# Slot-to-token combine weights made among the small experts and stored, instead of in the combine's turns

## What is computed

```python
logits = einsum('bmd,npd->bmnp', x, phi_n)              # token m, slot n*16+p
D = softmax(logits, axis=1)                             # over the tokens: what a slot reads
C = softmax(logits.reshape(b, m, n * p), axis=-1)       # over the slots: what a token reads back
Xs = einsum('bmd,bmnp->bnpd', x, D)
hdn = layernorm(Xs) @ w1 + b1; hdn = gelu(hdn); Ys = hdn @ w2 + b2
Y = einsum('bsd,bms->bmd', Ys, C); h = h + Y
```

## Time and profile before

| | us |
|---|---|
| median of 3 runs | 1556.29 |
| lowest, highest | 1554.89, 1559.04 |
| profiled execution, its own time | 1558.22 |
| span of that execution in the trace | 1556.5 |
| e0 with PE at work | about 400 to 928 |
| combine with PE at work | about 939 to 1391 |

### The profile page before, as it was taken

The page is one execution under the profiler, slowest core; times in us unless marked ns, Lnnn a source line. Parts: engine busy times, 40 slices in busy tenths (PEclk is TensorE's granted clock), DMA queues, the critical chain, the costliest instruction groups (busy, mean ns, idle before and its releaser), DMA issues. The chain is left out here.

```text
span 1556.5 us, 28510 instructions
## 1 busy us (share of the span) xinstructions
PE 1431.4 (92%) x8824; PEld 1269.1 (82%) x8824; DVE 978.6 (63%) x2877; ACT 891.0 (57%) x1833; POOL 270.8 (17%) x255
## 2 busy tenths in 40 slices
PE   3899999985899999999999986999999999957995
PEld 1577777774799999999999976999999999956985
DVE  6776666442777777777777744777776777632231
ACT  1377777774666666666666642655555555524551
POOL 5411100000111111111111101122121212120434
PEclk9999999998899999999999997889898989867998
DMA  7035655576466666666666654434333436105542
GB/s 198 25 123 146 146 135 135 140 172 149 136 200 186 193 189 196 187 190 197 189 189 190 199 155 148 129 108 126 114 125 99 121 116 190 31 11 148 134 91 20
DMA packets 202698, 220.87 MB, mean 142 GB/s; under 512 B 30065, under 2 KB 169528, under 8 KB 202606
## 3 DMA queue, kind: packets, MB, share of 16 engines
q1 hardware_dynamic: 170254, 179.96, 41.5%
q10 hardware_dynamic: 24672, 32.79, 6.2%
q0 software_dynamic: 7680, 6.95, 2.4%
HBM read 142.27 MB, written 79.90 MB: 143 GB/s over the span
## 5 line engine op out<-in xcount | busy, mean ns | idle before, releaser
L1062 PE MATMUL bank<-e_w,e_h_full 128*128 128x192 f32 x1920 | 324.5, 326 | 0.3
L1062 PEld LDWEIGHTS bank<-e_w,e_h_full 128*128 128x128 f32 x1920 | 310.6, 190 | 1.2 <-ACT e_h_full L1123 0.8
L1123 ACT ACTIVATE e_h_full<-bank,e_b 128x512 f32<-128x512 f32 x240 | 165.1, 689 | 196.7 <-PE bank L60 196.7
L1000 POOL TENSOR_TENSOR e_ln_rstd<-e_ln_var_eps,minus_half 128x4 f32<-128x4 f32 x64 | 64.8, 1013 | 524.2 <-DVE e_ln_var_eps L1173 524.2
L1180 DVE TENSOR_SCALAR e_rows<-e_slot_sums,e_ln_mean_var,e_ln_rstd 128x192 f32<-128x192 f32 x256 | 79.9, 376 | 76.2 <-POOL e_ln_rstd L1000 76.2
L1096 ACT ACTIVATE e_x_full<-bank,e_ln_shift,e_ln_gain 128x512 f32<-128x512 f32 x128 | 92.6, 773 | 53.3 <-PE bank L1035 48.5
L585 DVE TENSOR_REDUCE column_neg_max<-bank 128x4 f32<-128x512 f32 x64 | 44.3, 692 | 115.1 <-PE bank L60 103.7
L1351 POOL TENSOR_TENSOR ln_rstd<-ln_var_eps,minus_half 128x2 f32<-128x2 f32 (+1 forms) x35 | 51.8, 1481 | 345.5 <-DVE ln_var_eps L1652 345.5
L60 PE MATMUL bank<-e_x_hi,e_w1hi 128*128 128x512 f32 x240 | 105.4, 439 | 5.3 <-DVE e_w1lo L1159 3.5
L830 PE MATMUL bank<-x,dispatch_weights 128*128 128x193 f32 x512 | 97.0, 333 | 14.1 <-ACT slot_stage L690 13.5
L1412 PE MATMUL bank<-slot_out_and_one,combineT 128*128 128x193 f32 x512 | 94.5, 338 | 10.9 <-DMA slot_out_and_one<-slot_outputs 10.9
(11 more groups left out here) (214 smaller groups left out, 3071.5 us busy)
## 6 DMA issues: line engine op xcount, KB each, us to landing
slot_sums<-slot_stage SPq DMA_DIRECT2D x64, 386.0 KB
e_slot_sums<-slot_sums SPq DMA_DIRECT2D x64, 386.0 KB, 3.6
slot_outputs<-e_stage ACTq DMA_DIRECT2D x64, 384.0 KB, 3.4
slot_out_and_one<-slot_outputs SPq DMA_DIRECT2D x32, 768.0 KB
e_w<-in_w SPq DMA_DIRECT2D x64, 288.0 KB, 3.0
slot_logits<-kept_logits SPq DMA_DIRECT2D x64, 256.0 KB
slot_logits<-slot_logits SPq DMA_DIRECT2D x32, 512.0 KB, 3.4
e_w1raw<-in_w SPq DMA_DIRECT2D x80, 192.0 KB, 2.7
```

The source lines that it names most:

```text
L1000: pool.tensor_tensor(rs[u][:], ve[u][:], half[:], ALU.pow).then_inc(rstd_ready, 1)
L1062: last = pe.matmul(ybank(u)[:, j // 2, (j % 2) * D:(j % 2 + 1) * D], hf[:, k, js], w2s[u][:, k, :], start=k == 0, stop=k == MT - 1)
L1123: act.activation(hf[:, m, :], hbank(u, m), act_fn, bias=b1s[:, m, ds(n, 1)]).then_inc(acted, 1)
```

## The change

A new class `Weigher` makes the combine weights of batch i in round i of e0: SP loads logits and maxima one round ahead, DVE adds the negated maximum behind the outputs of the even expert, ACT takes the exponential at the end of its odd expert, and in the next round's even expert, behind `take_x`, ACT's queue stores the tile (512 KB) to a new tensor `T["cw"]`. All its tiles have one buffer. The combine loads the finished weights, into two buffers. The diff at its core:

```diff
+class Weigher:
+    def load(self, sp, b):
+        past(sp, self.less, b)
+        sp.dma_start(self.lg[:], self.T["lg"][ds(b, 1), :, :, :]...).then_inc(self.lg_in, 16)
+        sp.dma_start(self.nmb[:], self.T["nm_rows"][ds(b, 1), :]....partition_broadcast(P)).then_inc(self.lg_in, 16)
+
+    def less_max(self, dve, b):
+        dve.wait_ge(self.lg_in, 32 * b + 32)
+
+        past(dve, self.stored, 16 * b)
+        dve.tensor_tensor(self.cw[:], self.lg[:], self.nmb[:].unsqueeze(1).broadcast_to([P, NC, P]), ALU.add
+                          ).then_inc(self.less, 1)
+
+    def exp(self, act, b):
+        act.wait_ge(self.less, b + 1)
+        act.activation(self.cw[:], self.cw[:], ACT.Exp).then_inc(self.exped, 1)
+
+    def store(self, act, b):
+        act.wait_ge(self.exped, b + 1)
+        act.dma_start(self.T["cw"][ds(b, 1), :, :, :]..., self.cw[:]).then_inc(self.stored, 16)
...
 class CombineLoads:
     def sync(self, sp):
-        for u in range(3):
-            sp.wait_ge(self.T["kept_stored"][u], 16 * ((NG * NC + 2 - u) // 3))
-        sp.wait_ge(self.T["nm_stored"], 16 * NG)
+        sp.wait_ge(self.T["cw_stored"], 16 * 2)
         for b in range(2):
-            self.load_logits(sp, b)
+            self.load_weights(sp, b)
     def scalar(self, act):
         act.activation(self.Whi[:], self.Wraw[:], ACT.Copy).then_inc(self.W_hi_ready, 1)
-        act.wait_ge(self.C_ready, 1)
-        act.activation(self.cT[:], self.lg[0][:], ACT.Exp).then_inc(self.C_exp, 1)
     def vector(self, dve):
-        dve.wait_ge(self.lg_in[0], 32)
-        dve.tensor_tensor(self.lg[0][:], self.lg[0][:], ..., ALU.add).then_inc(self.C_ready, 1)
...
 expert_phase, SP:
+                    if weigh is not None and (not isinstance(i, int) or i + 1 < turns):
+                        weigh.load(sp, i + 1)
 expert_phase, ACT, at the end of each expert of a round:
+                        if weigh is not None and u == 1:
+                            weigh.exp(act, i)
+                        if weigh is not None and u == 0 and (not isinstance(i, int) or i > 0):
+                            weigh.store(act, i - 1)
 expert_phase, ACT, behind the last round:
                 send(n_exp - 1, 1)
+                if weigh is not None:
+                    weigh.store(act, turns - 1)
+                    act.wait_ge(weigh.stored, 16 * turns)
                 if then is not None:
                     then.scalar(act)
 expert_phase, DVE, behind the outputs:
+                        if weigh is not None and u == 0:
+                            weigh.less_max(dve, i)
...
 combine_phase:
-                def load_logits(b):
-                    past(sp, S["C_exp"], b - 1)
-                    early.load_logits(sp, b)
+                def load_weights(b):
+                    past(sp, S["Y_done"], b - 1)
+                    early.load_weights(sp, b)
-                        pe.wait_ge(S["C_exp"], y + 1)
+                        pe.wait_ge(cT_in[u], 16 * (y // 2 + 1))
-                    if n is not None:
-                        exp_combine(n)
-                    if n is not None:
-                        less_max(n)
```

More of the change, by code:

```diff
@@ L152, in tower_program @@
                 expert_phase(nc, T, "e0", small, T["ys"].rearrange("s b d -> (s b) d"), ins["b2_0"], ACT.Gelu, al,
-                             then=early)
+                             then=early, weigh=Weigher(Alloc(nc, c3), al, T))
                 tower_sems.free_sems()
@@ L210, in load_first_weights, with __init__, wait_logits @@
             self.load_w2(sp, u, u)
+class Weigher:
+    def __init__(self, sb_of, sem_of, T):
+        self.T = T
+        self.lg, self.nmb = sb_of.sb("weigh_logits", [P, NC, P]), sb_of.sb("weigh_neg_max_rows", [P, P])
+        self.cw = sb_of.sb("weigh_out", [P, NC, P])
+        self.lg_in, self.less, self.exped = sem_of.sem("weigh_logits_in"), sem_of.sem("weigh_less_max"), sem_of.sem("weigh_exp")
+        T["cw_stored"] = self.stored = sem_of.sem("weigh_stored")
+    def wait_logits(self, sp):
+        for u in range(3):
+            sp.wait_ge(self.T["kept_stored"][u], 16 * ((NG * NC + 2 - u) // 3))
+        sp.wait_ge(self.T["nm_stored"], 16 * NG)
+    def load(self, sp, b):
+        past(sp, self.less, b)
+        sp.dma_start(self.lg[:], self.T["lg"][ds(b, 1), :, :, :].rearrange("a p c t -> p (a c) t")).then_inc(self.lg_in, 16)
+        sp.dma_start(self.nmb[:], self.T["nm_rows"][ds(b, 1), :].rearrange("a t -> (a t)").partition_broadcast(P)
+                     ).then_inc(self.lg_in, 16)
+    def less_max(self, dve, b):
[8 more added lines that the diff above has]
+        act.wait_ge(self.exped, b + 1)
+        act.dma_start(self.T["cw"][ds(b, 1), :, :, :].rearrange("a p c t -> p (a c) t"), self.cw[:]).then_inc(self.stored, 16)
 class CombineLoads:
@@ L219, in __init__ @@
         self.T, self.ins = T, ins
-        self.lg = [sb(f"slot_logits{u}", [P, NC, P]) for u in range(2)]
-        self.nmb = [sb(f"token_neg_max_rows{u}", [P, P]) for u in range(2)]
+        self.cT = [sb(f"combineT{u}", [P, NC, P]) for u in range(2)]
         self.Wraw = sb("Wqkv", [P, 2, 3 * D])
@@ L225, in __init__, with load_weights @@
         self.rank, self.numbers = sb("rank", [P, NE1]), sb("token_numbers", [P, NB])
-        self.cT = sb("combineT", [P, NC, P])
         self.W_in, self.tables_in, self.router_in = sem("qkv_weights_in"), sem("attn1_tables_in"), sem("router_in")
-        self.lg_in = [sem(f"slot_logits_in{u}") for u in range(2)]
+        self.cT_in = [sem(f"combine_weights_in{u}") for u in range(2)]
         self.W_hi_ready, self.W_split = sem("W_hi_ready"), sem("W_split")
-        self.C_ready, self.C_exp = sem("C_ready"), sem("C_exp")
         self.Wp0, self.Wp1 = sb("Wproj0", [P, D]), sb("Wproj1", [DR + 1, D])
         self.rw0, self.rw1 = sb("router0", [P, NE1]), sb("router1", [P, NE1])
-    def load_logits(self, sp, b):
-        sp.dma_start(self.lg[b % 2][:], self.T["lg"][b]).then_inc(self.lg_in[b % 2], 16)
-        sp.dma_start(self.nmb[b % 2][:], self.T["nm_rows"][b, :].partition_broadcast(P)).then_inc(self.lg_in[b % 2], 16)
+    def load_weights(self, sp, b):
+        sp.dma_start(self.cT[b % 2][:], self.T["cw"][b]).then_inc(self.cT_in[b % 2], 16)
     def sync(self, sp):
@@ L869, in past, with expert_phase @@
             eng.wait_ge(sem, value)
-def expert_phase(nc, T, name, L, dst, b2, act_fn, sem_of, routed_to=None, then=None):
+def expert_phase(nc, T, name, L, dst, b2, act_fn, sem_of, routed_to=None, then=None, weigh=None):
     n_exp, hid, MT, src, ln = L.n_exp, L.hid, L.MT, L.src, L.ln
@@ L985, in _ @@
                 load_rows(3, 1)
+                if weigh is not None:
+                    weigh.wait_logits(sp)
+                    weigh.load(sp, 0)
                 each_pair(sp, turn)
@@ L1411, in turn @@
                         for c in range(NC):
-                            last = pe.matmul(bank[:, 0, 0:D + 1], cT[:, c, :], ysb[u][:, c, :],
+                            last = pe.matmul(bank[:, 0, 0:D + 1], cT[u][:, c, :], ysb[u][:, c, :],
                                              start=c == 0, stop=c == NC - 1)
@@ L1500, in _ @@
             def _(act):
-                def exp_combine(b):
-                    act.wait_ge(S["C_ready"], b + 1)
-                    past(act, S["Y_done"], b)
-                    act.activation(cT[:], lg[b % 2][:], ACT.Exp).then_inc(S["C_exp"], 1)
                 def turn(t, u, n, y, q, a, p, r, z, w):
@@ L1563, in _ @@
                 st = Steps(dve, steps)
-                def less_max(b):
-                    dve.wait_ge(lg_in[b % 2], 32 * (b // 2 + 1))
-                    dve.tensor_tensor(lg[b % 2][:], lg[b % 2][:], nmb[b % 2][:].unsqueeze(1)
-                                      .broadcast_to([P, NC, P]), ALU.add).then_inc(S["C_ready"], 1)
                 def choose(r):
```

14 lines of the change are left out of this document (7 added, 7 removed).

## The result

The changed kernel takes 1681.64 us (median of 4 runs, 1678.95 to 1684.8) against 1557.64 for the kernel before (4 runs): ratio 1.0799 [1.0772, 1.0826]. A second set of runs gave 1677.95 (6 runs) against 1564.66 (21 runs): 1.075 [1.071, 1.079]. The change makes the kernel slower by 7.5 to 8%. The forecast was 1663, with 1628 to 1710 as its range.

A forecast was written before the change was run, and what follows sets the result against it. PE was taken to bound both e0 and the combine. Terms 78 + 26 + 3 = 107 us on the profiled 1558.22 gave 1665, or 1663 us for a median lying 1.9 lower; range 1628 to 1710.

The forecast's parts named there:

- The chain over ACT: e0: two table loads and the exponential on ACT delay PE's third part 2.5 us in 31 rounds, 78 us.
- The clock: e0: half of PE's new waits pull its clock down, 1.7 us lost each; 26 us, bounds 0 and 53.
- The combine: Combine's turns: the removed addition and exponential both have cover, so nearly nothing is gained; 0 to -3 us, taken as 0.
- its own condition: Combine: the prediction calls itself wrong if the combine's length changes by more than 5 us.
- The bound: Combine: if all PE's idle time came back, the gain would be 389.00 - 385.56 = 3.4 us.
- The end of e0: End of e0: `Wqkv_hi` stands behind the last store's landing, moving the combine's first loads 2.4 to 4 us; 3 taken.
- The addition and the store: e0, DVE: addition covered by the longer round (5 us without it); store landing taken as 4.0 us, so 0.
- the first rival: e0: ACT's table loads delay PE, with the clock falling in some rounds; 1634 to 1690 us, chance 0.62.
- the second (the store): e0: the store's landing decides; at 5 us 31 more, 1694, at 5.5 us 1710; chance 0.18.
- the third (a switch that costs more than its load): e0, ACT: the engine must first run empty; at twice 1.28 us a switch, 213 more, 1769 us; chance 0.05.
- The fourth (loads that hide): e0: one of the two loads runs while ACT waits for PE; 1596 us, up to 1630; chance 0.10.
- The fifth: Faster: ACT's waiting swallows the added work, the combine loses the exponential ahead of `x4T_hi`, 34 less, 1525 us; chance 0.03.

The follow-up runs named there:

- the fill experiment: Changed kernel with 5 more 128x512 matmuls, results unused, on PE in its wait between second and third part of the even expert: 1648.56 us, e0 612.1.
- the second profile: The changed kernel as it is, profiled again in a second set of runs: median 1677.95 us, e0 657.3.
- the second tile: Changed kernel with a tile of its own for the differences, so DVE's addition no longer waits for the store: 1677.38 us, e0 657.1.
- the small exponential: Changed kernel with e0's exponential on 128 of the 1024 numbers of a partition, both table loads a round kept: 1603.02 us, e0 593.4.

## Why the forecast held, and where its sum was off

The step that decided, two table loads and the exponential between two experts with PE's third part behind them, is shown: the loads are at their place, the wait is there 31 times, without loads it all but goes (5.3 us in 16 waits), and it shrinks with a shorter exponential by what that saves. The terms, against the earlier trace rows and the table of stages:

- **The chain over ACT: 78 us forecast, 72 to 75 measured.** 75.4 by the fill experiment, 119.3 - 47.7 = 71.6 in the changed kernel. A round loses 2.3 to 2.4 us where 2.5 was said. The 0.1 us in it for a matmul behind a wait was read from rows without one; behind the waits it is about right (0.50 to 0.53 us against 0.40).
- **The clock: 26 forecast, 44 to 50 measured.** This is the term that was mis-sized. 97 us at the lower level are 48.7 lost, 1.0 of which was there before; 50 in the second profile; 43.9 by the fill. The price of a fall (1.7 us, from the earlier trace rows) was right, the count wasn't: "half of the waits" are nearly all. The row of 4.54 us at one end and the idle 1.17 us in a window of 4 at the other leave 2.2 us open. The runs fill it: in them the clock fell behind no wait of up to 1.6 us, and behind nearly every one of 2.0 us or more.
- **The combine: 0 forecast (0 to -3), -7.8 and -6.4 measured, 7 of it at equal clock.** This step failed, and its own condition (a change of more than 5 us) says so. "The addition runs while POOL takes its power, and DVE still waits behind it" was read as cover for every turn, but the earlier trace rows have that wait only 16 times. In the turns that place tokens DVE has no wait behind the addition, so all of it delays what follows, and those turns take 11.79 us with it and 11.25 without: 6.5 us in 13. (The exponential's cover held: the combine is 469.5 us without it.) The bound was wrong as well, since the earlier trace rows cover 389 of the stage's 468.6 us: in all of it PE is busy for 433.79 us, so idle for 34.8, and for 431.37 of 460.8 us in the changed kernel, so idle for 29.4. Of the 7.8 us, 5.4 were PE's idle time. These are its only waits between 962 and 1342 us of the kernel before; they stand in the turns that place tokens and vanish without the addition:

```profile
PE bank L60 <- ACT oT L1511: 3.2, 10, 0.4
```

- **The end of e0: 3 forecast, 2.4 measured**, by the mechanism named.
- **The addition and the store: 0 forecast, 0 measured** (657.1 us with two tiles against 656.0), with more room than was said: the landing is 2.6 us, not 4.0. The addition without the longer round was put at 5 us; with a copy for the exponential 11.9 us were left, and the store's wait is among them.

By these, 107 should have been 114 (119.3 + 2.4 - 7.8). That the sum comes so near is in part luck: the clock was put 22 us too low, the chain and the combine 14 us too high. The spans of the two profiled executions differ by 124.9 us, and the 11 beyond 114 are the later start; for the medians of the first runs, 124.0 apart, that isn't shown, as one execution of each has a trace. Two smaller figures were off: the range's lower end of 1628 lies below the 1634 that the first rival gives, and 5 us isn't what a measurement tells, as later runs of the kernel before lie between 1553 and 1573 us.

Of the rivals, the second (the store) is out by the second tile, and the third (a switch that costs more than its load) by the loads themselves: at most 0.02 us at either side of them in ACT's rows, so the drain that the Trainium skill states in "ScalarE: Activation LUTs", section "What ACT_TABLE_LOAD costs", shows in none of the 31 rounds either. The fourth (loads that hide) doesn't happen, because ACT has no wait between the two loads. The fifth had the right stage for a gain, a combine that gets faster, and the wrong instruction: without the exponential the combine is as long as before.

## What to carry to other kernels

Price a new wait on PE twice, once for its length and once for the clock behind it: here 75 and 44 us, and 1.3 us of useless matmuls in each wait gave the second back. Don't put functions of two tables into one loop that PE waits on. Before calling a wait cover for an instruction, count in how many turns the wait stands (here in every second one), and look at what follows the instruction in the others.

## What was unexpected of the hardware

- POOL's 128x2 power takes 1.58 us beside DVE's 128x1024 addition and 0.71 without it, and the profile shows all of it as busy time.
- In e0 PE's clock fell behind 28 of the changed kernel's 29 waits of 2.1 to 2.2 us, each time for 3.4 us. It fell behind no wait of up to 1.6 us, there or with the small exponential, and behind none of those of 1.0 us with added matmuls before them.
- PE's first products run at about half speed for a time that changes from execution to execution. The same eight matmuls of the changed kernel, in its first profile and then in its second:

```profile
60.85 7.87 PE L60 MATMUL bank<-xT,M 128*128 128x512 f32 x8 [0.68 <-ACT xT L664]
```

```profile
60.10 4.18 PE L60 MATMUL bank<-xT,M 128*128 128x512 f32 x8 [0.68 <-ACT xT L664]
```

The trace's entries of the granted clock begin at 90.1 us in the first and at 57.8 us in the second, at the higher level, and a stretch without entries counts as 1.00 in the views. So the slow products fit a clock that is still at its lower level. In all 13 profiles the two go together: in 9 the entries begin at 56 to 58 us and e0 at 388 to 392, in 4 at 89 to 93 us and e0 at 400 to 408. Why the clock rises at the one time or the other isn't shown.
